# Graph attention in fp32: one chunk of four heads' probabilities transposed through DRAM, and a new order of TensorE's work in a slot

## The reference

```python
def attention(h, adj, Wq, bq, Wk, bk, Wv, bv, beta):      # 64 batches, N=128 rows, D=384, 12 heads of 32
    q, k, v = split_heads(h @ Wq + bq), split_heads(h @ Wk + bk), split_heads(h @ Wv + bv)
    scores = einsum('bhqd,bhkd->bhqk', q, k) / sqrt(32) + beta * adj[:, None]
    scores = where(adj[:, None] > 0, scores, -9e15)
    return einsum('bhqk,bhkd->bhqd', softmax(scores), v)   # heads joined again

h = maximum(layernorm(x), 0)
out = x + attention(h, adj, ...)
```

## Time and profile before

| | |
|---|---|
| median of 3 runs | 534.79 us (534.7 to 534.97) |
| profiled execution: its time, its span | 535.0 us, 533.1 us |
| PE busy (matmuls) | 520.9 us, 98% |
| DVE busy | 451.9 us, 85% |
| ACT busy | 462.3 us, 87% |
| POOL busy | 127.3 us, 24% |
| TensorE clock granted | 1.000, which is 2.4 GHz throughout |
| DMA packets | 75.25 MB in 89671 packets, a mean of 141 GB/s |

### The profile page before, as it was taken

The page is one execution under the profiler, slowest core; times in us unless marked ns, Lnnn a source line. Parts: engine busy times, 40 slices in busy tenths (PEclk is TensorE's granted clock), DMA queues, the critical chain, the costliest instruction groups (busy, mean ns, idle before and its releaser), DMA issues.

```text
span 533.1 us, 17434 instructions
## 1 busy us (share of the span) xinstructions
PE 520.9 (98%) x5394; PEld 438.7 (82%) x5394; DVE 451.9 (85%) x2285; ACT 462.3 (87%) x1856; POOL 127.3 (24%) x204
## 2 busy tenths in 40 slices
PE   8989999999999999999999999999999999999995
PEld 8768888888888888888888888888888888888774
DVE  6788998888898898898888889888889987765896
ACT  3558899999999999999999999998998999888984
POOL 4522222212212222221221222222122111101211
PEclk9999999999999999999999999999999999999999
DMA  7523374654646465464645556364565434222111
GB/s 238 186 81 91 115 215 123 201 154 133 192 137 188 123 170 176 123 192 140 189 134 149 177 143 192 128 188 133 138 189 161 128 116 123 71 80 75 51 56 46
DMA packets 89671, 75.25 MB, mean 141 GB/s; under 512 B 39056, under 2 KB 86288, under 8 KB 89616
## 3 DMA queue, kind: packets, MB, share of 16 engines
q1 hardware_dynamic: 89616, 74.62, 46.5%
HBM read 40.37 MB, written 34.21 MB: 140 GB/s over the span
## 4 chain that ended last, share of the span: by engine, by line
PE 90%; DVE 2%; issue 1%; DVEq 0%
PE G_ps L797 35%; PE S_ps L868 18%; PE PT_ps L852 17%; PE S_ps L817 10%; PE PT_ps L834 9%; DVE probsT L682 1%; DVE probs L651 0%; PE G_ps L852 0%; PE PT_ps L858 0%; DVE outT L634 0%; PE S_ps L878 0%; DVE y L701 0%; PE S_ps L894 0%; DVE y L669 0%; DVE qk L621 0%
## 5 line engine op out<-in xcount | busy, mean ns | idle before, releaser
L481 ACT ACTIVATE probs<-probs,negmax 128x128 f32<-128x128 f32 x768 | 298.1, 397 | 0.1
L651 DVE CUSTOM_DVE_ANT_0 probs<-S_ps,bias 128x128 f32<-128x128 f32 x768 | 164.2, 283 | 3.3 <-PE S_ps L817 3.3
L481 ACT ACTIVATION_READ_ACCUMULATOR probs<-probs,negmax 128x1 f32 x768 | 150.2, 196 | 0.0
L452 POOL TENSOR_TENSOR y<-y,x_ring 128x384 f32<-128x384 f32 x63 | 63.4, 1007 | 343.6 <-DVE y L669 343.6
L797 PE MATMUL G_ps<-h_hi,w_lo 128*128 128x512 f32 x288 | 117.7, 409 | 0.0
L797 PE MATMUL G_ps<-h_hi,w_hi 128*128 128x512 f32 x288 | 117.7, 409 | 0.0
L797 PE MATMUL G_ps<-h_lo,w_hi 128*128 128x512 f32 x288 | 116.2, 403 | 0.0
L489 ACT COPY probsT<-PT_ps 128x512 f32<-128x512 f32 x181 | 99.9, 584 | 12.0 <-PE PT_ps L852 11.4
L852 PE MATMUL PT_ps<-ident,probs 128*128 128x128 f32 x728 | 103.6, 277 | 0.0
L852 PEld LDWEIGHTS PT_ps<-ident,probs 128*128 128x128 f32 x728 | 81.9, 141 | 10.3 <-issue 1.0
L868 PE MATMUL S_ps<-w_hi,h_hi 128*128 128x384 f32 x192 | 65.2, 339 | 0.0
(11 more groups left out here) (57 smaller groups left out, 603.6 us busy)
## 6 DMA issues: line engine op xcount, KB each, us to landing
out_dram<-y SPq DMA_DIRECT2D x63, 192.0 KB, 1.9
x_ring<-in_x_dram SPq DMA_DIRECT2D x15, 768.0 KB, 5.4
out_rows<-out_blocks SPq DMA_DIRECT2D x58, 192.0 KB, 1.9
out_moved<-out_rows SPq DMA_DIRECT2D x232, 48.0 KB, 2.1
xhat_rows<-xhat_blocks SPq DMA_DIRECT2D x26, 384.0 KB, 2.6
xhat_moved<-xhat_rows SPq DMA_DIRECT2D x104, 96.0 KB, 2.7
adj_in<-in_adj_dram SPq DMA_DIRECT2D x16, 256.0 KB, 3.2
x_ring<-in_x_dram SPq DMA_DIRECT2D x4, 192.0 KB, 3.2
```

The lines of the kernel that those rows point to most:

```text
L452: nc.gpsimd.tensor_tensor(y[:, z.s % 2 ^ d, :], y[:, z.s % 2 ^ d, :], x_ring[:, bass.ds(at, D)], ALU.add).then_inc(y_ready, 1)
L481: last = nc.scalar.activation(p, p, ACT.Exp, bias=negmax[:, e, j * KC + m:j * KC + m + 1], scale=TURN, accum_out=rowsum[:, e, m * HC + j:m ...
L651: last = nc.vector.tensor_tensor_reduce(probs[:, a, j, m, :], S_ps[:, j, m * N:(m + 1) * N], bias[(z.par + 1) % 2][:, z.s, :], 1.0, LARGES ...
```

## The change

Three things are done to the steady state. The first chunk of each batch (heads' chunk m = 0) no longer goes over PE: ACT does its exponentials one slot ahead, in the slot of the scores, straight into `probs_blocks`; SP writes them to DRAM, reads them back in the next slot in four pieces, and DVE transposes 32x32 blocks into `probsT[:, 0]`. PE's order in slots 1 to 3 becomes `scores(a)`, stretch 1, `probs_times_v(o)`, `values(a)`, `transpose_probs` 1 and 2, stretch 2; slot 0 keeps the products first. `scores` waits for `h_lo_stored` only in the groups where PE still transposes x and in the slot right after them. Beside that the store of unit 2 goes from DVE to ACT, x comes in four loads of one batch instead of one of four, DVE's mask stands ahead of `store_outT` in slots 1 to 3, and the start (loads, warm-ups, order of the low parts) and the tail (who copies which chunk) are arranged anew.

```diff
+LOADS = [[0], [1, 2], [3], []]
...
-STORE_V = [[], [2], [], [5]]
+STORE_0 = [[], [], [2], []]
+STORE_V = [[], [], [], [5]]
-WARM = [8, 4, 4, 6, 8]
+WARM = [8, 2, 2, 3, 7]
...
+        FOUR = HC * HD
+        probs_blocks = sb("probs_blocks", [P, HC * FOUR])
+        probs_rows = nc.dram_tensor("probs_rows", [2, P, HC * FOUR], F32, kind="Internal").ap()
+        probs_moved = sb("probs_moved", [P, 2, HC * FOUR])
...
+                self.R = self.E and not self.F
+                self.Q = self.A and self.P and not (n == NG - 1 and s == GROUP - 1)
+                self.scores_first = self.A and self.P and s > 0
...
-            for q in range(2):
+            for q in range(GROUP):
                 load_first(q)
             load_weights(0, wq, 0, P, w_first)
-            for q in range(2, GROUP):
-                load_first(q)
...
 # SP, in slot(z), in this order
+                if z.R:
+                    sp.wait_ge(probs_rows_written, 16 * (z.e + 1))
+                    for c in range(HC):
+                        came = probs_rows[(z.s - 1) % 2, :, c * FOUR:(c + 1) * FOUR].rearrange("(r p) n -> p r n", r=HC)
+                        goes = probs_moved[c * HD:(c + 1) * HD, (z.s - 1) % 2, :].rearrange("p (r n) -> p r n", r=HC)
+                        sp.dma_start(goes, came).then_inc(probs_blocks_moved[(z.s - 1) % 2], 16)
                 if z.W:
                     sp.wait_ge(outT_stored, z.o + 1)
                     sp.dma_start(out_rows[z.s % 2, :, :], out_blocks[:, :]).then_inc(out_rows_written, 16)
...
+                if z.Q:
+                    sp.wait_ge(probs_ready[0], z.a + 1)
+                    sp.dma_start(probs_rows[z.s % 2, :, :], probs_blocks[:, :]).then_inc(probs_rows_written, 16)
...
+                if z.T and z.s == 1:
+                    if started(z.groups(0)):
+                        sp.wait_ge(bias_ready, z.count(0) - 1)
+                    sp.dma_start(adj_in[(z.par + 1) % 2][:, :, :],
+                                 adj_v[:, bass.ds(z.groups(1), 1), :, :].rearrange("q g s k -> q (g s) k")).then_inc(adj_loaded[(z.par + 1) % 2], 16)
+                if not (z.static and z.groups(3) >= NG):
+                    if z.s == 0:
+                        sp.wait_ge(stats_ready, z.count(1) + 2)
+                    for q in LOADS[z.s]:
+                        sp.dma_start(x_ring[:, bass.ds(z.ring(3, q), D)],
+                                     x_v[:, bass.ds(z.groups(3), 1), q, :].rearrange("t g d -> t (g d)")).then_inc(x_loaded[(z.par + 1) % 2], 16)
...
 # ACT
+            def exponentials_ahead(z):
+                act.wait_ge(masked, z.a + 1)
+                if started(z.a - 1):
+                    act.wait_ge(rinv_ready, z.a - 1)
+                if started(z.a):
+                    act.wait_ge(probs_rows_written, 16 * z.a)
+                a = z.s % 2
+                blocks = probs_blocks.rearrange("p (c j e) -> p j c e", c=HC, j=HC)
+                for j in range(HC):
+                    last = nc.scalar.activation(blocks[:, j, :, :], probs[:, a, j, 0, :].rearrange("p (c e) -> p c e", c=HC), ACT.Exp,
+                                                bias=negmax[:, a, j * KC:j * KC + 1], scale=TURN, accum_out=rowsum[:, a, j:j + 1])
+                last.then_inc(probs_ready[0], 1)
...
+                if z.Q:
+                    exponentials_ahead(z)
                 if z.E and not z.F:
                     store_probsT(z, 1)
...
 # DVE
+            def transpose_probs(z):
+                dve.wait_ge(probs_blocks_moved[(z.s - 1) % 2], 64 * (z.moved_before() + 1))
+                if started(z.e):
+                    dve.wait_ge(pv_done, z.e)
+                nc.vector.transpose(probsT[:, 0, :].rearrange("p (j r e) -> p r j e", j=HC, r=HC),
+                                    probs_moved[:, (z.s - 1) % 2, :].rearrange("p (r j e) -> p r j e", r=HC, j=HC)).then_inc(pT_stored[0], 1)
...
+                if z.O and not z.F:
+                    reciprocals(z)
+                if z.scores_first:
+                    mask(z)
                 if z.O:
                     store_outT(z)
...
                 if z.A:
                     add_bv(z)
+                if z.R:
+                    transpose_probs(z)
...
 # PE
-                pe.wait_ge(h_lo_stored, z.t)
+                if z.X or z.M and z.s == 0:
+                    pe.wait_ge(h_lo_stored, z.t)
...
-                if z.O:
+                if z.A and z.scores_first:
+                    scores(z)
+                if z.O and not z.scores_first:
                     probs_times_v(z)
-                if z.A:
+                if z.A and not z.scores_first:
                     scores(z)
-                if z.E:
-                    transpose_probs(z, 0)
                 if z.P:
                     for part in STRETCH_1[z.s]:
                         project(z, *part)
+                if z.O and z.scores_first:
+                    probs_times_v(z)
                 if z.A:
                     values(z)
```

More of the change, by code:

```diff
@@ L517, in slot @@
                 if z.E:
-                    exponentials(z, 0)
+                    if z.F:
+                        exponentials(z, 0)
                     exponentials(z, 1)
-                    if not (z.F and not z.A):
+                    if z.F and z.A:
                         store_probsT(z, 0)
+                if z.P:
+                    for u in STORE_0[z.s]:
+                        store_qk(z, u)
+                if z.E:
                     exponentials(z, 2)
+                    if z.F and not z.A:
+                        store_probsT(z, 2)
                 if z.P:
@@ L533, in slot @@
                     store_probsT(z, 2)
+                if z.M:
+                    high_part(z)
                 if z.P:
-                    for u in STORE_2[z.s]:
+                    for u in STORE_2[z.s] + STORE_V[z.s] * (z.static and z.groups(0) == 0):
                         store_qk(z, u)
-                if z.X and z.P and not z.A:
+                if z.X and z.P and not z.between:
                     high_part(z)
@@ L615, in store_qk @@
                 if u < KC:
-                    if z.static and z.groups(0) == 0:
+                    if z.static and z.groups(0) == 1:
                         dve.wait_ge(bq_ready, 1)
@@ L721, in slot @@
                     mask(z)
+                if z.O and not z.F:
+                    reciprocals(z)
+                if z.scores_first:
+                    mask(z)
                 if z.O:
                     store_outT(z)
+                if z.A and not z.F and not z.scores_first:
+                    mask(z)
                 if z.M:
@@ L727, in slot @@
                     normalise(z, q)
-                if z.O:
+                if z.F and z.O:
                     reciprocals(z)
-                if z.A and not z.F:
-                    mask(z)
                 for d in z.moved:
@@ L765, in slot @@
                     normalise(z, q)
-                if z.P:
+                if z.P and not first:
                     for u in STORE_V[z.s]:
                         store_qk(z, u)
+                if first and z.s == GROUP - 1:
+                    weights_low(8)
             all_slots(slot)
@@ L871, in transpose_xhat @@
             def transpose_xhat(z):
-                pe.wait_ge(xhat_ready, z.t + 1)
+                pe.wait_ge(xhat_ready, order(z.t) + 1)
                 if z.A:
@@ L936, in slot @@
                     transpose_probs(z, 1)
-                if z.X and z.A:
+                if z.X and z.P and z.between:
                     transpose_xhat(z)
```

131 lines of the change are left out of this document (65 added, 66 removed).

## The result

The changed kernel takes 547.3 us (median of 4 runs, 545.23 to 548.69) against 534.88 of the kernel before beside it: a ratio of 1.023, 95% interval 1.0189 to 1.0272. The forecast was 520.9. One of the four runs of the kernel before took 605.17 us and is left out of the ratio. The profiled execution took 548.69 us with a span of 546.5, against 535.0 and 533.1: 13.4 us more span.

A forecast was written before the change was run, and what follows sets the result against it. PE alone bounds the kernel before; after, SP's circle decides in groups 2 to 12. Gains of 7.5 there, 3.4 in groups 13 to 15, start 1.5, groups 0 and 1 0.9, tail 0.6 give 13.9: 520.9 us, range 513 to 532.

The forecast's parts named there:

- the circle: SP's queue followed once round, from slot 0's probs write through DVE and ACT to the next: 30.75 us; chance 0.44.
- The three signs: Prediction wrong if DVE never waits for probs, a read set issues clearly under 1.7 us, or reads land after 3.
- I take 30.7 for the groups 2 to 12: Groups 2 to 12 each take 30.7 us instead of 31.38, 7.5 us gained over eleven groups.
- The sum is 3.5 + 8.15 + 7.6 + 3.5 + 3.6 + 4.4 = 30.75 us: Legs of SP's round: slots 0, 1, 2, slot 3's reads, DVE to the mask, then ACT; longer than PE's 30.24.
- The longer circle: Rival: steady groups at 31.2 to 31.8 us, total 526 to 533; chance 0.13.
- The end of the circle: In slot 0's scores PE stands some 0.5 us per group on DVE's store of unit 5.
- The start and group 0: Start gains 1.5 us, from 0 to 2.0; groups 0 and 1 lose two waits of 2.5, less 0.5 for unit 5.
- Groups 13 to 15: Loads of x end there, PE's 30.24 us holds: three groups gain 1.14 each, 3.4 us.
- PE's own 30.24: PE's work per group: 31.38 less 1.68 for transposes plus 0.54 for order changes, from 29.7 to 30.8 us.
- The tail: In the last slots ACT takes one of DVE's three copies: 0.6 us gained, bounds 0 and 1.2.
- The Trainium skill's rule: By the page SP's issuing would not count and steady groups would all take 30.24 us; the prediction disagreed.
- The slower rival: Probs' reads land after 3.8 us behind loads of x, the circle is 32.4, total 539.6 us; chance 0.12.

The follow-up runs named there:

- e16: e13 with group 1's two xhat_rows writes moved to the ends of slots 2 and 3, first pair's reads to slot 3: 530.56 us, 0.9899.
- e13: e9 with x in four loads of 192 KB, two each in slots 1 and 3 behind the probs' write, not one of 768 KB: 534.4 us, 0.9959.
- e7: Changed kernel with the edits of e5 and e6 together; blocks land in wrong places: 530.14 us, 0.9905.
- e6: Changed kernel with out_moved and xhat_moved read in two DMAs a set, not four, same bytes; blocks in wrong places: 532.76 us, 0.9943.
- e9: e8 with slot 3's output store issued by SP again, those of slots 0 to 2 still by ACT: 533.83 us, 0.9956.
- e10: e8 with all output stores issued by SP: 540.0 us, 1.0096.
- e5: Changed kernel without slot 0's wait for h's low part in the loop, and unit 5 stored before slot 3's low part: 545.25 us, 1.0193.
- e12: Kernel before, scores no longer waiting for h's low part except in slot 0 and the first groups: 535.19 us, 0.9993.
- e15: Kernel before with one extra 128x512 block transpose on DVE in every slot, nobody waiting for it: 536.08 us, 1.0016.
- e3: Changed kernel with x in one load of 768 KB in slot 3, four groups ahead, not four of 192 KB: 541.41 us, 1.0098.
- e1: Changed kernel with the probs read in one DMA, not four, same bytes; blocks in wrong places: 548.57 us, 1.0233.
- e11: Changed kernel with the probs read in two DMAs, not four, same bytes; blocks in wrong places: 540.53 us, 1.0089.
- e8: Changed kernel with e5's edit, x in one load in slot 3, group 1's probs write before its xhat write, output stores issued by ACT: 540.32 us, 1.0118.

## Why the prediction was wrong, point by point

The mechanism was the one named, SP's in-order queue and the circle through it. Two terms of the sum failed, about equal in size: the length of the circle (10.9 us over groups 4 to 12), and groups 1 to 3 (11.5 us), a place that the sum hardly looked at. The three signs that the prediction named for being wrong all failed to appear: DVE does wait for the probs, a set of reads issues in 1.8 us and lands after 2.3. They tested the mechanism and not its sizes.

*"I take 30.7 for the groups 2 to 12": groups 2 and 3 were taken as steady.* Per group this is the step that failed most. Predicted for group 1 was 1.1 us lost, bounds 0 and 2, and for 2 and 3 together 1.4 gained. Measured: 2.7 and 8.5 lost. The prediction listed each wait of SP in the steady state but didn't follow its queue through group 1, where PE still transposes x and DVE has the batch for `xhat_rows` only at the slot's end. Before, SP had nothing behind that write that anyone was waiting for; now the probs' write and reads stand behind it. e16 moved nothing but the DMAs of `xhat_rows` and `xhat_moved` in that group and is 3.8 us below e13 by the medians, with the intervals just apart; so this is shown for a third of the 11.2 us, and weakly. A second part is SP's long issues, which the prediction put at nothing: 5.0 us in groups 2 and 3 of the changed kernel, where the chain lies on SP. How much of them reaches the time was not tested, nor why they are long. That the lateness lasts into group 3 fits the next point: a queue whose round is as long as the group can't catch up. Where the round was shortened (e7), group 3 took 31.3 for 34.6.

*"The sum is 3.5 + 8.15 + 7.6 + 3.5 + 3.6 + 4.4 = 30.75 us".* Right in kind, too short. From 235.86 to 267.47 the same circle takes 31.61:

| leg | predicted | measured |
|---|---|---|
| SP, slot 0, write to the next reads | 3.5 | 239.49 - 235.86 = 3.63 |
| SP, slot 1 | 8.15 | 247.93 - 239.49 = 8.44 |
| SP, slot 2 | 7.6 | 255.83 - 247.93 = 7.90 |
| slot 3's reads until landed | 3.5 | 259.32 - 255.83 = 3.49 |
| DVE, transpose to slot 0's mask | 3.6 | 262.98 - 259.32 = 3.66 |
| mask, exponentials, to the write | 4.4 | 267.47 - 262.98 = 4.49 |

0.72 of the 0.86 us lie in the legs of SP. The four reads of `out_rows` with the pause behind them took 1.97 to 2.10 us for the 1.8 summed, and from a write of `out_rows` to its reads it was 2.20 for 1.9; a load of x took 0.5 where 0.8 was summed. The groups 4 to 12 took 31.9 on average where 30.7 was forecast and 31.38 is the break-even: 10.9 us. With 0.7 us between the forecast circle and break-even, an error of 3% turned the sign. e6 shows that it is the issuing: 3.9 us less of it a group, at equal bytes and with the work of the other engines unchanged, gained 14.5 us although the reads landed later. e9 against e10 shows the same with the shape of every transfer kept. The longer circle was a rival at 31.2 to 31.8 with a chance of 0.13; it came out just beyond, and with the rest of the sum as forecast it would have left the kernel about even.

*The end of the circle.* The prediction had PE stand on DVE's store of unit 5. It stands on DVE's transpose of the probs (0.25 us, ahead of the products) and on the low part (0.65), which slot 0's scores still wait for in every group of the loop: the code has `z.X or z.M and z.s == 0`, while the words of "The change" have only the slot right after the groups with flag X. All wait for the same late DVE, and taking the wait on the low part away brought at most 2 us (e5).

*The start and group 0.* 3.5 us gained were forecast ahead of the first scores (1.5, and 2.0 of the waits less unit 5), 0.2 measured in the profiled run. In the runs' profiles the first scores lie between 26.1 and 31.9 us, with the same code ahead of them in several. In e16's, the latest, PE stood 3.17 us for `xhat` up to 21.03 and the granted clock was 0.50 from 21 to 27, where projections followed each other after 0.43 us for 0.23 at 1.00; what made `xhat` late, and what moves the others, is left open.

*What held.* The wait on `h_lo` was worth nothing by itself (e12), a transpose more on DVE in every slot cost about a microsecond there (e15), and SP's issues by themselves took the 1.8 and 0.4 us that were summed.

*Groups 13 to 15.* Forecast 3.4 gained, measured 1.5: group 13 took 31.87, and it holds 4.5 us of long issues. That it had to make up for a late queue doesn't explain it: in e16 the groups 8 to 11 ran at 30.36, and group 13 took 32.64, with 4.0 us of long issues. Group 14's 30.37 and e13's and e16's 30.36 bear out PE's own 30.24. *The tail*: 0.6 forecast, 0.8 measured.

*The Trainium skill's rule.* In the Trainium skill, "DMA: Bandwidth & Descriptors", section "Issuing engines are not separate DMA queues", calls the time to start a DMA usually small relative to the DMA. In this kernel it isn't small: 1.8 us of issuing a set beside 2.3 of landing, and cutting the count of DMAs at equal bytes gave 2.7% (e6). The same section's other half, that several issuing engines save this sequencer time, is borne out by e9 against e10: 6 us.

*The slower rival.* It forecast 539.6 by reads that land late behind loads of x. In the changed kernel the reads land after 2.3 us, so this is not its cause. Where x came in one large load (e3, e9) it did happen, in the slot behind that load; in e13, with loads of a quarter, slot 1 was back at 7.76. The changed kernel's four loads cost SP 1.3 us of issuing a group instead; e3, with both effects against each other, came out 6 us ahead.

In sum: ahead of group 1 3.3, group 1 1.6, groups 2 and 3 9.9, groups 4 to 12 10.9, groups 13 to 15 1.9, tail -0.2, outside the span 0.3: 27.7 us between the forecast change (-13.9) and the measured one (+13.7).

What stays open: a set of four takes 1.8 us on average, but some take 2.9 to 3.8. Every kernel has them, nearly all of them ahead of group 4 and from group 12 on. Before, SP's waits hid them; after, the queue has no slack. What makes them was not tested, and neither was what makes the runs of the changed kernel spread over 3.5 us. The granted clock goes with it in part: in e13 and e16 the longer runs are those with the lower clock, and in the profiles of e3, e9 and e16 stalls of PE came ahead of its fall; in the changed kernel's four runs the two don't go together (548.69 us at 0.998, 546.89 at 0.992).

## What to carry to other kernels

An engine that only issues DMAs has a length of work like any other: add up its instructions from the trace (here 0.34 to 0.43 us each, 0.53 to 0.61 for a block read into 128 partitions) with the pauses between them, and compare the round with the period before you give it more. Allow for some tenths too little in every leg: a queue without slack has no way to make up for one late item. Follow an in-order queue through the irregular first groups as well, look for issues that are long where code runs for the first time, and put a DMA that waits for something late behind those that others wait for. When an experiment takes issues away, measure the new ones and their landing too: one read for four (e1) gave everything back, two for four (e6, e11) a part.

## What the runs showed of the hardware

- One DMA of 256 KB in 512 pieces lands after 3.4 us and the DMA behind it after 3.1; the same pieces in two land after 2.8, in four after 2.3, the last issued 1.35 after the first (e1, e11, after). From the first issue to the last landing it is 3.4, 3.4 (0.6 + 2.8) and 3.65 us: for the reader alone the split hardly matters, for the queue it does.
- A block read into 128 partitions cost SP 0.53 us of issuing (e1) to 0.61 (e6, e11), one into 32 partitions 0.43 (after), so halving the number of DMAs saved a third of the issuing and not half.
- SP's issues that took over 0.5 us more than their kind lie in the loop's first pass and in code that is written out: in the changed kernel 5 in groups 2 and 3 and 9 in groups 12 to 15, none in the eight groups between. The cause is not shown.
- ACT stood 4.08 us, released by nothing in the profile, behind a DMA that it issued at the very end of its loop's body, and 3.7 to 4.4 us each time, once for each return to the loop's start; with that one moved to SP and three in earlier slots kept, the pause went (e8, e9).
- Small reads (64 KB) issued 1.0 us behind a load of 768 KB landed some 6 us after their issue (e9, group 6); its other steady groups lost less in that slot, 0.1 to 1.4 us.
- Where PE had stood idle for 1.01 and 1.27 us in e9, the granted clock fell from 1.00 to 0.50 and small matmuls that follow each other after 0.17 us took 0.32 each (201.49 against 225.63 to 226.84): the stall cost more than its wait.
